# Layer 0's state-space scan in steps of 1024 elements, with B broadcast from DRAM and one shared decay bank

## The chip, the cores and the metric

The program runs on one NeuronCore of a Trainium2 chip. A core has five engines with an instruction stream each: TensorE (PE in the profile, its weight loads PEld), VectorE (DVE), ScalarE (ACT), GpSimd (POOL) and SyncE (SP, which here only issues transfers). They meet through semaphores. Operands lie in SBUF, and in PSUM, which has 8 banks of 128 x 512 float32. The metric is the time of one execution in microseconds (us), the lower the better.

## What is computed

The reference is a network of four layers on 4096 tokens (16 sequences of 256) of width 128. The change touches layer 0 alone, which adds a selective state-space scan and a mixture of experts to its input. The scan, cut to what matters:

```python
deltaA = jnp.exp(jnp.einsum('bld,dn->bldn', delta, A))          # decay
deltaB_u = (delta * u)[..., None] * Bm[:, :, None, :]           # input
def step(h, t):
    dA_t, dBu_t, C_t = t
    h = dA_t * h + dBu_t
    return (h, jnp.einsum('bdn,bn->bd', h, C_t))
y = ys + u * D
y = y * silu(res)
return y @ W_out + b_out
```

There are 256 channels d, 16 states n and 256 steps of time per sequence. The mixture sends each token to 2 of 16 experts with a capacity of 512; 12 of the experts are networks 128 to 512 to 128 with an exact GELU, and the results are gathered by token, weighted and added.

## The kernel before

Channels lie on the 128 partitions, in two halves c = 0, 1; time lies along the free axis. The function `mamba_front` (lines 338 to 588) makes u, delta, the gate (parked in DRAM as `gate_d`), and B and C for all tokens as three bf16 parts stacked on 96 partitions (`bc3`, the tile `bc` of the profile). Its last work is a row of scatters of tokens to the experts' buffers by GpSimd, the last seven of which wait for the logarithms of ScalarE (`ln_done`).

The function `mamba_scan` (lines 601 to 1021) walks over `NQ` = 128 steps q: 16 sequences b, and in each 8 pairs of states. A step has two units i, one for each half of the channels; a unit is 512 elements wide, 256 of time for each of the two states. For a unit

- ScalarE writes the decay to one of three PSUM banks (`decay`, L883), two instructions of 255 elements, since the first element of each state is 0 and makes the scan start anew;
- GpSimd multiplies delta*u by the spread B into `bu` (L746, a ring of 3), from `b_sb`, into which ScalarE has copied (L893) what TensorE spread over the partitions (L770) from the bf16 parts with a selection matrix;
- VectorE scans (L970) and multiplies by C (L976, tile `hc`), which TensorE has spread to bank 3 (L779);
- TensorE adds `hc` to the output's bank with an identity (L794, float32).

At the end of a sequence VectorE multiplies by the gate (L983), and TensorE projects (L807) and adds the residual (L808). The order of each engine's instructions is written out by hand, and the experts lie in the gaps of the same streams: expert e begins at step 7 + 6e (`FIRST`, `SPACING`), with a transposition (L845), two pairs of first-layer products (L837), each pair followed by its two GELUs on ScalarE (L914), the second layer (L820) and an addition by VectorE (L989). A GELU needs another activation table than the decay's exponential, so each pair of GELUs costs a table load before it and one after it. From step 84 on GpSimd also fetches 64 blocks of expert results by index (L731), nearly two a step; ScalarE weighs them (L924) and VectorE adds them (L999). SyncE issues the loads of weights, tokens and gates and the stores of results.

Both functions are printed here:

Of the kernel before, what the change touches and what calls it, by code (L numbers as in the profile page):

```python
# [6 lines left out]
F32 = mybir.dt.float32  # L7
# [330 lines left out]
def mamba_front(nc, g, t, u, gate_d, delta, bc3, r, disp, ybuf, scattered, f):  # L338
# [10 lines left out]
    with section(nc, "front", *ROUTE, "xz_ready", "gate_ready", "gate_out0", "gate_out1", "act_done", "biased",  # L349
                 "b_out_in", "near_in", "delta_in", "dt_ready", "dtx_done", "z_ready", "zb_done", "high_done", "rem_done",  # L350
                 "copied", "split_done", "abs_done", "exp_done", "ln_done", "delta_done", "neg_a") as s:
# [7 lines left out]
        rem = s.sb("rem", [KBC, 2, CH])  # L359
        with ExitStack() as early:  # L360
# [4 lines left out]
        gate_out = (s.gate_out0, s.gate_out1)  # L365

# [15 lines left out]
        with nc.Block() as block:  # L382

            @block.sync
            def _(sp):
                for dst, src in ((w_dt_in, "m_w_dt_in"), (w_bc, "m_w_bc"), (w_dt, "m_w_dt"), (b_dt, "m_b_dt")):
                    sp.dma_start(dst[:], t[src]).then_inc(s.delta_in, 16)
# [8 lines left out]
                for b in range(BATCH):  # L396
                    sp.wait_ge(s.gate_ready, b + 1)
                    sp.dma_start(gate_d[:, :, b * T:(b + 1) * T], gate[:, b % 2]).then_inc(gate_out[b % 2], 16)
                for p in range(2):
                    sp.wait_ge(gate_out[p], BATCH // 2 * 16)  # L400
                sp.wait_ge(s.near_in, 64)
# [199 lines left out]
def mamba_scan(nc, g, t, u, gate_d, delta, bc3, sel, disp, ybuf, r, scattered, f):  # L601

    PAIRS = DS // 2
    NQ = BATCH * PAIRS
    NU = NQ * DC
    DA, C_BANK, E0_BANK, BO, Y_BANK, E1_BANK = 0, 3, 4, 5, 6, 7
    RING = 3
    NE, CT = E0 - FIRST_MLP0, CAP0 // P
    W2, B1, B2, WN = FC * P, 2 * FC * P, 2 * FC * P + FC, 2 * FC * P + FC + D
    FIRST, SPACING = NT - SCATTERED_IN_FRONT + 3, 6  # L610
    TURN, UP0, UP1, DOWN0, DOWN1 = 0, 2, 4, 6, 7
    A_TURN, A_UP0, A_UP1 = 2, 4, 6
    GRP, SLOTS = 4, 4
    NGRP = NT // GRP
    Q_GATHER = FIRST + SPACING * (NE - 1) + 11
    Q_LAST = NQ - 3
    SKIP_BY_ACT = Q_GATHER // PAIRS + 1
    names = [f"gathered{j}" for j in range(NGRP)]
    with section(nc, "scan", *names, "skip_made", "skip_used", "zeroed", "du_ready", "b_ready", "b_copied", "bu_made",
                 "da_ready", "scan_done", "c_ready", "hc_ready", "sum_done", "yg_ready", "o_ready", "o_taken",  # L620
                 "gate_in0", "gate_in1", "ew_in0", "ew_in1", "ex_in0", "ex_in1", "turned", "xt_ready", "h_ready",
                 "act_done", "y_ready", "y_out", "stored", "weighted0", "weighted1", "combined") as s:
        a_neg, d_col, w_out = f.a_neg, f.d_col, f.w_out
        skip = s.sb("skip", [P, DC, T])
        exp_centre = s.sb("exp_centre", [P, 1])
        du = s.sb("du", [P, 2, DC, T])
        hc = s.sb("hc", [P, RING, 2, T])
        yg = s.sb("yg", [P, DC, T])
        gate = s.sb("gate", [P, 2, DC, T])
# [5 lines left out]
        free = g.xn_t[:].rearrange("p (k n t) -> p k n t", n=2, t=T)  # L635
        bu, b_sb, h = free[:, 0:3], free[:, 3:5], free[:, 5:7]
        gb = g.xn[:].rearrange("p (j k i) d -> p j k i d", j=SLOTS, k=2)
        gathered = s.sems[:NGRP]
        weighted, weighted_bank = (s.weighted0, s.weighted1), (E0_BANK, E1_BANK)
        gate_in, ew_in, ex_in = (s.gate_in0, s.gate_in1), (s.ew_in0, s.ew_in1), (s.ex_in0, s.ex_in1)  # L640

        def bank(i):
            return g.ps[:, i, :].rearrange("p (n t) -> p n t", t=T)
# [4 lines left out]
        def phase(q, offset):  # L648
            e, rest = divmod(q - FIRST - offset, SPACING)
            return e if rest == 0 and 0 <= e < NE else None  # L650

        def due(q):
            if q < Q_GATHER:
                return 0
            return min(2 * NT, -(-(q - Q_GATHER + 1) * 2 * NT // (Q_LAST - 4 - Q_GATHER)))

        def combined_at(q):
            return range(due(q - 3) // (2 * GRP), due(q - 2) // (2 * GRP)) if 0 <= q < NQ else range(0)

        last_groups = range(due(NQ - 3) // (2 * GRP), NGRP)  # L660

        with nc.Block() as block:

            @block.sync
            def _(sp):
                def load_gate(b):
                    if b >= 2:
                        sp.wait_ge(s.yg_ready, b - 1)
                    sp.dma_start(gate[:, b % 2], gate_d[:, :, b * T:(b + 1) * T]).then_inc(gate_in[b % 2], 16)
# [16 lines left out]

                load_gate(0)
                load_gate(1)
                load_weights(0)
                load_weights(1)  # L690
                sp.wait_ge(scattered, 2 * NT * 16)
                load_tokens(0)
                load_tokens(1)
                for q in range(NQ):
                    b, pr = divmod(q, PAIRS)
                    e = phase(q, TURN + 1)
                    if e is not None and e + 2 < NE:
                        load_tokens(e + 2)
                    e = phase(q, DOWN1 + 2)
# [4 lines left out]
                    if b >= 1 and pr == 2 and b + 1 < BATCH:  # L704
                        load_gate(b + 1)

            @block.gpsimd
            def _(pool):
                nc.gpsimd.memset(exp_centre[:], EXP_CENTRE).then_inc(s.zeroed, 1)

                def inputs(b):
                    to = slice(b * T, (b + 1) * T)
                    nc.gpsimd.tensor_tensor(du[:, b % 2], delta[:, :, to], u[:, :, to], ALU.mult).then_inc(s.du_ready, 1)

                def skip_term(b):
                    if b >= 1:
# [2305 lines left out]
```

## Time and profile before

| | |
|---|---|
| time, median of 3 runs | 1978.54 us (1978.04 to 1988.57) |
| span of the profiled execution, first to last instruction | 2006.6 us |
| what lies around that span | not recorded apart; the profiled span is itself 1.4% above the median |
| the scan's stage in the span | 179.4 to 792.9 us |
| DVE, PE, ACT, POOL busy in the whole span | 64%, 79%, 53%, 40% |
| mean granted TensorE clock | 0.890 |

The profile shows one execution. Busy time is the sum of an engine's instructions, and idle time is given with what ended it. In the trace a float32 matmul appears as two records, so 1024 records of L794 are 512 matmuls. The clock is a fraction of 2.4 GHz.

### The profile page before, as it was taken

What the parts mean: (1) busy time and instruction counts of PE and PEld (TensorE: products, weight loads), DVE (VectorE), ACT (ScalarE), POOL (GpSimd) and SP (SyncE); (2) the same over time, 40 slices, a digit from 0 to 9 for tenths busy, and PEclk for the clock granted to TensorE, in tenths of its full rate; (3) what the DMA queues carried; (4) which work ended last, traced back from release to release, by engine and by line L of the source; (5) the groups of instructions that cost most, each with busy time, mean ns of one, the idle gap of its engine ahead of it and who ended that gap; (6) DMA issues with size and microseconds to landing.
All of it is one profiled execution on the core that took longest, in us unless ns stands there. A gap on an engine that the chain in (4) does not pass through costs nothing. (4 is left out here: it accounts for less than half of the span.)

```text
span 2006.6 us, 34124 instructions
## 1 busy us (share of the span) xinstructions
PE 1593.7 (79%) x12145; PEld 1087.2 (54%) x12146; DVE 1288.1 (64%) x2309; ACT 1058.9 (53%) x1931; POOL 797.6 (40%) x809
## 2 busy tenths in 40 slices
PE   5993788888876776758889998965799999749974
PEld 5661566666654445535567765542344444638863
DVE  7525888788788888764534457758753896724334
ACT  1345787887776764434434444545454777314421
POOL 1447766565669994374212234431400000150041
PEclk9996899999998889658989999987699999569987
DMA  5211011111001110665321124314531341211311
GB/s 151 89 56 44 22 50 56 35 49 50 28 20 35 30 29 23 229 182 88 64 57 59 59 57 81 63 25 131 103 67 42 50 67 17 95 49 51 100 43 55
DMA packets 153335, 130.56 MB, mean 65 GB/s; under 512 B 18929, under 2 KB 137864, under 8 KB 152914
## 3 DMA queue, kind: packets, MB, share of 16 engines
q1 hardware_dynamic: 140554, 104.54, 21.1%
q0 software_dynamic: 12544, 23.82, 4.3%
q8 instruction: 100, 1.64, 0.4%
q14 instruction: 65, 0.53, 0.1%
q10 hardware_dynamic: 72, 0.03, 0.0%
HBM read 77.08 MB, written 52.43 MB: 65 GB/s over the span
## 5 line engine op out<-in xcount | busy, mean ns | idle before, releaser
L746 POOL TENSOR_TENSOR xn_t<-xn_t,scan_du 128x512 f32<-128x512 f32 x256 | 320.9, 1271 | 154.9 <-ACT xn_t L893 105.1
L970 DVE TENSOR_TENSOR_SCAN xn_t<-banks,xn_t 128x512 f32<-128x512 f32 x256 | 311.5, 1217 | 78.7 <-ACT banks L883 42.0
L794 PE MATMUL banks<-scan_hc,ident 128*128 128x256 f32 x1024 | 295.4, 414 | 49.1 <-DVE scan_hc L976 49.1
L2417 ACT ACTIVATE att_pr<-banks 128x768 f32<-128x768 f32 (+1 forms) x256 | 234.3, 917 | 161.9 <-PE banks L2309 76.1
L883 ACT ACTIVATE banks<-delta,scan_exp_centre,a_neg 128x255 f32<-128x255 f32 x512 | 265.0, 559 | 14.8 <-DVE xn_t L970 14.4
L794 PEld LDWEIGHTS banks<-scan_hc,ident 128*128 128x128 f32 x1024 | 193.7, 207 | 110.2 <-DVE scan_hc L976 70.1
L976 DVE TENSOR_TENSOR scan_hc<-xn_t,banks 128x512 f32<-128x512 f32 x256 | 175.8, 687 | 33.4 <-PE banks L779 14.3
L1030 POOL DMA_INDIRECT disp<-xn_tok,places x128 | 135.3, 1057 | 154.6 <-ACT att_pr L2417 44.2
L2325 PE MATMUL banks<-att_pr,att_vx 128*32 128x256 f32 (+1 forms) x2048 | 163.6, 383 | 19.0 <-issue 9.3
L2458 DVE TENSOR_REDUCE att_mb<-banks 128x6 f32<-128x768 f32 x128 | 121.1, 954 | 89.5 <-PE banks L2283 48.7
L2462 DVE TENSOR_REDUCE att_mb<-banks 128x4 f32<-128x1024 f32 x128 | 153.9, 1221 | 18.5 <-PE banks L2276 13.4
L2276 PE MATMUL banks<-att_ks,att_qs 48*128 48x256 bf16 (+1 forms) x1024 | 118.1, 281 | 45.0 <-DMA att_ks<-k_parts 31.2
L893 ACT COPY xn_t<-banks 128x512 f32<-128x512 f32 x128 | 74.5, 582 | 123.7 <-PE banks L770 92.2
L2301 PE MATMUL banks<-att_qs,att_ks 50*128 50x256 bf16 (+1 forms) x1024 | 111.0, 272 | 13.2 <-DMA att_qs<-att_mt 11.0
L1231 POOL IOTA gau_rev<- 128x8 f32 x1 | 0.1, 138 | 302.2 <-POOLq L76 302.2
L1415 POOL DMA_DIRECT2D ybuf<-att_yo x72 | 38.8, 539 | 156.7 <-DVE att_yo L1400 153.1
L1316 PE MATMUL banks<-grouped_w,att_xt 128*128 x288 | 98.4, 465 | 0.5 <-DVE att_xt L1382 0.3
L1605 POOL DMA_INDIRECT gau_gb<-ybuf,rows x32 | 32.2, 1007 | 146.0 <-DMA ybuf<-gau_eyo 136.6
L1365 ACT ACTIVATE att_a<-banks 128x352 f32<-128x352 f32 x72 | 33.4, 463 | 104.8 <-PE banks L1316 104.8
L2276 PEld LDWEIGHTS banks<-att_ks,att_qs 48*128 48x128 bf16 x1024 | 50.1, 101 | 64.2 <-issue 28.5
L779 PE MATMUL banks<-bc,state_sel 96*128 96x256 bf16 x256 | 53.0, 290 | 34.4 <-DVE scan_hc L976 27.7
L2325 PEld LDWEIGHTS banks<-att_pr,att_vx 128*32 128x32 f32 x2048 | 43.5, 110 | 66.0 <-issue 40.7
(384 smaller groups left out, 3339.2 us busy)
## 6 DMA issues: line engine op xcount, KB each, us to landing
scan_ew<-f_packed SPq DMA_DIRECT2D x12, 578.0 KB
q_parts<-att_p_parts SPq DMA_DIRECT2D x16, 384.0 KB, 4.7
k_parts<-att_p_parts SPq DMA_DIRECT2D x16, 384.0 KB, 6.1
att_qs<-q_parts SPq DMA_DIRECT2D x64, 96.0 KB
att_ks<-k_parts SPq DMA_DIRECT2D x64, 96.0 KB
gau_ew<-f_packed SPq DMA_DIRECT2D x8, 578.0 KB
disp<-zeros SPq DMA_DIRECT2D x1, 4608.0 KB, 15.4
att_xin<-disp SPq DMA_DIRECT2D x72, 64.0 KB
```

Of the source, the lines that this page charges most:

```text
L746: nc.gpsimd.tensor_tensor(bu[:, i % RING], b_sb[:, q % 2], du[:, b % 2, c:c + 1, :].to_broadcast([P, 2, T]), ALU.mult).then_inc(s.bu_made, 1)
L794: ins = nc.tensor.matmul(bank(Y_BANK)[:, c, :], g.ident[:], hc[:, i % RING, n, :], start=False, stop=(i % (PAIRS * DC) == PAIRS * DC - 1 a ...
L883: ins = nc.scalar.activation(bank(DA + i % RING)[:, n, 1:T], delta[:, c, b * T + 1:(b + 1) * T], ACT.Exp, scale=a_neg[:, c, state:state + ...
L970: v.tensor_tensor_scan(rows(h[:, i % 2]), g.ps[:, DA + i % RING, :], rows(bu[:, i % RING]), 0.0, ALU.mult, ALU.add).then_inc(s.scan_done, 1)
L976: v.tensor_tensor(hc[:, i % RING], h[:, i % 2], bank(C_BANK), ALU.mult).then_inc(s.hc_ready, 1)
L1030: pool.indirect_dma_start(disp, bass.IndirectOffsetOnAxis(ap=r.scat_i[:, k, i:i + 1], axis=0), src[:, i, :], None, bounds_check=disp.shape ...
L2276: ins = nc.tensor.matmul(g.ps[:, 2 * m_slot(i) + half, lo:hi], qs[rows_of, p, j, q * P:(q + 1) * P], ks[rows_of, p, j, 0:hi - lo], start=T ...
L2301: ins = nc.tensor.matmul(g.ps[:, 2 * s_slot(i) + half, k * T:k * T + T - q0], ks[rows_of, p, j, k * P:(k + 1) * P], qs[rows_of, p, j, q0:T ...
L2325: ins = nc.tensor.matmul(g.ps[r * 32:(r + 1) * 32, O_BANK, q0:T], vx[:, b % 2, k, 4 * jg + r, :], pr[:, i % RING, half, k * T:k * T + T - q0],
L2417: nc.scalar.activation(pr[:, i % RING], g.ps[:, at:at + 2, 0:W], ACT.Exp, scale=scale).then_inc(s.p_ready, 1)
L2458: v.tensor_reduce(mb[:, b % 2, j, :].rearrange("p (g n) -> p g n", g=2), g.ps[:, at:at + 2, 0:W].rearrange("p g (n k) -> p g n k", k=P), A ...
L2462: v.tensor_reduce(mb[:, b % 2, j, :], g.ps[:, at:at + 2, :].rearrange("p g (n k) -> p (g n) k", k=T), AX_X, ALU.max).then_inc(s.m_taken, 1)
```

## The change

The steps are cut the other way. A step k of 128 now is one state for two sequences (`PASS` = 512 columns of time) and for both halves of the channels at once, 1024 elements wide, in 8 passes of 16 states. One scan, one product with C, one product of GpSimd and two decays of 2 x 255 elements serve a step, where before there were two, two, two and four.

- B no longer goes through TensorE and ScalarE. The front copies the float32 rows of B from PSUM (`b_row`, one more ScalarE copy for each of 8 chunks) and SyncE stores them to `b_d` in DRAM. In the scan SyncE loads row n for each step, broadcast to 128 partitions (256 KB, 128 such loads, a ring of 4).
- C is still spread by TensorE from its bf16 parts, in one matmul of 512 columns; VectorE reads it for both halves with a step of 0.
- A step's two decays need two adjacent banks. Even steps use banks 0 and 1, odd ones banks 1 and 2, so bank 1 is shared: its decay for step k+1 waits until scan k is over, and scan k+1 waits for it. The other decay is made a step ahead.
- The skip term u*D is added by TensorE with a diagonal matrix (L801), in place of products on GpSimd and ScalarE and one on TensorE (L787).
- The experts are spaced 4 steps apart. The first two hidden blocks are parked in SBUF with `Identity` and get their GELU together with the other two, so that one table round trip serves an expert. The bias of the second layer is a matmul with a row of ones (L874), and ScalarE takes the result out (L928), not VectorE.
- The fetches are one a step, at steps 57 to 120; the weighted rows stay in SBUF, TensorE adds them (L835, L839), and ScalarE takes the sums out.

The core of the diff:

```diff
+                def store_b(ch):
+                    sp.wait_ge(s.b_saved, ch + 1)
+                    sp.dma_start(b_d[:, cols(ch)], b_row[:, ch % 2, :]).then_inc(b_out_done[ch % 2], 16)
...
                 def high(ch):
                     act.wait_ge(s.dt_ready, ch + 1)
+                    if ch >= 2:
+                        act.wait_ge(b_out_done[ch % 2], ch // 2 * 16)
+                    nc.scalar.copy(b_row[:, ch % 2, :], g.ps[0:DS, bc_bank(ch), :]).then_inc(s.b_saved, 1)
...
+    FIRST, SPACING = 7, 4
...
+                def load_b(k):
...
+                    if k >= B_RING:
+                        sp.wait_ge(s.bu_made, k - B_RING + 1)
+                    sp.dma_start(b_sb[:, k % B_RING, :], b_d[n:n + 1, cols(p)].to_broadcast([P, PASS])
+                                 ).then_inc(b_in[k % B_RING], 16)
...
+                    pool.wait_ge(b_in[k % B_RING], (k // B_RING + 1) * 16)
+                    if k >= BU_RING:
+                        pool.wait_ge(s.scan_done, k - BU_RING + 1)
+                    nc.gpsimd.tensor_tensor(bu[:, k % BU_RING], du[:, p % 2],
+                                            b_sb[:, k % B_RING, None, :].to_broadcast([P, DC, PASS]),
+                                            ALU.mult).then_inc(s.bu_made, 1)
...
+                    if GATHER <= k < GATHER + 2 * NT:
+                        fetch(k - GATHER)
...
+                def sum_states(k):
...
+                    pe.wait_ge(s.hc_ready, k + 1)
+                    for c in range(DC):
+                        ins = nc.tensor.matmul(g.ps[:, Y_BANK + c, :], g.ident[:], hc[:, k % 2, c, :], start=False,
+                                               stop=(n == DS - 1))
...
-                    for n in range(2):
-                        state = 2 * pr + n
-                        ins = nc.scalar.activation(bank(DA + i % RING)[:, n, 1:T], delta[:, c, b * T + 1:(b + 1) * T],
-                                                   ACT.Exp, scale=a_neg[:, c, state:state + 1], bias=exp_centre[:])
...
+                    bank = 2 * (k % 2) if own else SHARED
+                    c = bank - k % 2
+                    free_after = k - 1 if own else k
+                    if free_after >= 1:
+                        act.wait_ge(s.scan_done, free_after)
...
+                for k in range(NK):
+                    decay(k, False)
+                    decay(k + 1, True)
+                    if k >= 1:
+                        expert(k - 1)
...
+                    dve.wait_ge(s.da_ready, 2 * k + 2)
+                    dve.wait_ge(s.bu_made, k + 1)
+                    v.tensor_tensor_scan(rows(h[:, k % 2]), da_pair(k), rows(bu[:, k % BU_RING]), 0.0, ALU.mult,
+                                         ALU.add).then_inc(s.scan_done, 1)
```

ScalarE around one expert, before. `scan_eht` are the hidden blocks and `scan_ext` the transposed tokens; L883 is the decay, L893 the copy of B:

```order
L905 COPY scan_ext<-banks 128x512
L883 ACTIVATE banks<-delta,scan_exp_centre,a_neg 128x255 x2
L893 COPY xn_t<-banks 128x512
L883 ACTIVATE banks<-delta,scan_exp_centre,a_neg 128x255 x6
L897 COPY x_tok<-banks 128x256
L893 COPY xn_t<-banks 128x512
L914 ACT_TABLE_LOAD
L914 ACTIVATE scan_eht<-banks,scan_ew 128x512 x2
L883 ACT_TABLE_LOAD
```

The same place in the changed kernel. L913 is the decay, L941 the parked blocks, L947 and L950 the GELUs, L928 the expert's result:

```order
L934 COPY scan_ext<-banks 128x512
L913 ACTIVATE banks<-delta,scan_exp_centre,a_neg 128x2x255 x2
L941 ACTIVATE scan_eht<-banks,scan_ew 128x512 x2
L913 ACTIVATE banks<-delta,scan_exp_centre,a_neg 128x2x255 x2
L947 ACT_TABLE_LOAD
L947 ACTIVATE scan_eht<-banks,scan_ew 128x512 x2
L950 ACTIVATE scan_eht<-scan_eht 128x1024
L913 ACT_TABLE_LOAD
L913 ACTIVATE banks<-delta,scan_exp_centre,a_neg 128x2x255 x2
L928 COPY scan_eyo<-banks 128x512
```

Both tables are now loaded once per expert, with three GELUs between the loads where there were two; the next decays stand behind the second load.

TensorE over one expert in the changed kernel (L792 spreads C, L809 adds the states, L851 transposes, L863 and L869 are the first layer, L874 and L878 the second):

```order
L792 MATMUL banks<-bc,state_sel 128x512
L809 MATMUL banks<-scan_hc,ident 128x512 x2
L851 MATMUL banks<-ident,scan_exin 128x128 x4
L792 MATMUL banks<-bc,state_sel 128x512
L809 MATMUL banks<-scan_hc,ident 128x512 x2
L863 MATMUL banks<-scan_ext,scan_ew 128x512 x2
L792 MATMUL banks<-bc,state_sel 128x512
L809 MATMUL banks<-scan_hc,ident 128x512 x2
L869 MATMUL banks<-scan_ext,scan_ew 128x512 x2
L792 MATMUL banks<-bc,state_sel 128x512
L809 MATMUL banks<-scan_hc,ident 128x512 x2
L874 MATMUL banks<-scan_ew,ones_row 128x512
```

The sixteen matmuls of L878 follow. The whole expert stands within four steps, where before its pieces were spread over eight, the last two of them beside the next expert's first.

GpSimd in the gather phase of the changed kernel (L774 is the product with B, L758 a fetch, L748 a piece of delta*u):

```order
L774 TENSOR_TENSOR scan_bu<-scan_du,xn_t 128x1024
L758 DMA xn_tok<-ybuf,rows 128x128
L774 TENSOR_TENSOR scan_bu<-scan_du,xn_t 128x1024
L748 TENSOR_TENSOR scan_du<-delta,u 128x512
L758 DMA xn_tok<-ybuf,rows 128x128
```

One fetch stands behind each product, over 64 steps.

## Rows read from the trace of the kernel before

**Rows 1.** Windows of the stage with the scans alone: length, DVE busy (count), clock, DMA

```profile
275.00:560.00 285.00, 144.50 (x119) 0.96 0.14 43
580.00:767.00 187.00, 95.02 (x78) 0.87 0.11 29
767.00:789.00 22.00, 13.36 (x11) 1.00 0.00 1
```

**Rows 2.** The page's costliest groups that belong to the scan

```profile
L746 POOL TENSOR_TENSOR xn_t<-xn_t,scan_du 128x512 f32<-128x512 f32 x256 | 320.9, 1271 | 154.9 <-ACT xn_t L893 105.1
L970 DVE TENSOR_TENSOR_SCAN xn_t<-banks,xn_t 128x512 f32<-128x512 f32 x256 | 311.5, 1217 | 78.7 <-ACT banks L883 42.0
...
L883 ACT ACTIVATE banks<-delta,scan_exp_centre,a_neg 128x255 f32<-128x255 f32 x512 | 265.0, 559 | 14.8 <-DVE xn_t L970 14.4
...
L976 DVE TENSOR_TENSOR scan_hc<-xn_t,banks 128x512 f32<-128x512 f32 x256 | 175.8, 687 | 33.4 <-PE banks L779 14.3
...
L893 ACT COPY xn_t<-banks 128x512 f32<-128x512 f32 x128 | 74.5, 582 | 123.7 <-PE banks L770 92.2
```

**Rows 3.** Groups by form over the whole span: other widths, GELUs, table loads

```profile
L2000 DVE TENSOR_TENSOR att_p_rem<-att_p_y,att_p_parts 128x1024 f32<-128x1024 f32 x16 | 19.4, 1216 | 7.0 <-issue 3.9 <-ACT att_p_parts L2032 3.1
...
L2881 POOL TENSOR_TENSOR w_taps<-w_in_sb,w_taps 128x1024 f32<-128x1024 f32 x1 | 2.3, 2338 | 7.1 <-DMA w_taps<-m_taps 7.1
...
L2417 ACT ACTIVATE att_pr<-banks 128x1024 f32<-128x1024 f32 x128 | 130.6, 1023 | 49.1 <-PE banks L2301 47.4
...
L914 ACT ACT_TABLE_LOAD x24 | 30.8, 1283 | 0.4
...
L914 ACT ACTIVATE scan_eht<-banks,scan_ew 128x512 f32<-128x512 f32 x48 | 30.3, 683 | 0.3
```

**Rows 4.** Timeline at the stage's end, VectorE: start, us, engine, line

```profile
783.23 1.22 DVE L970 TENSOR_TENSOR_SCAN xn_t<-banks,xn_t 128x512 f32<-128x512 f32 x1
...
785.09 1.22 DVE L970 TENSOR_TENSOR_SCAN xn_t<-banks,xn_t 128x512 f32<-128x512 f32 x1
...
788.19 0.69 DVE L976 TENSOR_TENSOR scan_hc<-xn_t,banks 128x512 f32<-128x512 f32 x1
...
792.49 0.37 ACT L897 COPY x_tok<-banks 128x256 f32<-128x256 f32 x1 [8.81 <-PE banks L808]
```

**Rows 5.** Timeline of one pair of GELUs, ScalarE and VectorE

```profile
329.45 1.26 ACT L914 ACTIVATE scan_eht<-banks,scan_ew 128x512 f32<-128x512 f32 x2
...
330.74 1.28 ACT L883 ACT_TABLE_LOAD   x1
...
332.03 1.05 ACT L883 ACTIVATE banks<-delta,scan_exp_centre,a_neg 128x255 f32<-128x255 f32 x2
...
333.12 1.22 DVE L970 TENSOR_TENSOR_SCAN xn_t<-banks,xn_t 128x512 f32<-128x512 f32 x1 [1.36 <-ACT banks L883]
```

**Rows 6.** Timeline of TensorE at full clock (starts give the pace)

```profile
402.28 0.38 PE L779 MATMUL banks<-bc,state_sel 96*128 96x256 bf16 x2
402.50 1.03 PE L794 MATMUL banks<-scan_hc,ident 128*128 128x256 f32 x4
403.37 0.38 PE L770 MATMUL banks<-bc,state_sel 96*128 96x256 bf16 x2
```

**Rows 7.** Timeline of GpSimd: a fetch behind a product

```profile
641.29 1.04 POOL L731 DMA_INDIRECT xn_tok<-ybuf,rows  x1 [0.16 <-issue]
```

**Rows 8.** Timeline at the end of the front and the stage's start

```profile
172.96 0.97 POOL L1030 DMA_INDIRECT disp<-xn_tok,places  x1 [0.30 <-issue]
...
183.94 1.22 DVE L970 TENSOR_TENSOR_SCAN xn_t<-banks,xn_t 128x512 f32<-128x512 f32 x1 [4.36 <-POOL xn_t L746]
```

**Rows 9.** Loads by line: KB each, median us to landing

```profile
scan_exin<-disp SPq DMA_DIRECT2D x12, 256.0 KB, 2.9
```

**Rows 10.** The broadcast load of `b_out`, 64 KB, by its tile

```profile
DMA to landing us min/median/max: 3.9/3.9/3.9
```

More of the change, by code:

```diff
@@ L620, in mamba_scan @@
+    TURN, UP0, UP1, DOWN = 0, 1, 2, 3
+    GELUS = 3
+    GRP, SLOTS = PASS // P, 4
+    PROJECT = 3
+    STORED_AFTER = 2
+    GATHER = FIRST + SPACING * (NE - 1) + DOWN + 3
+    WEIGH = GATHER + 2 * GRP + 2
+    SCATTERED_HERE = NT - SCATTERED_IN_FRONT
+    names = [f"gathered{j}" for j in range(NPASS)]
+    with section(nc, "scan", *names, "zeroed", "diag_made", "du_ready", "b_in0", "b_in1", "b_in2", "b_in3", "bu_made",
                  "da_ready", "scan_done", "c_ready", "hc_ready", "sum_done", "yg_ready", "o_ready", "o_taken",
@@ L755, in _ @@
                         scatter(nc, pool, scattered, g.xn, disp, r, 2, range(i, i + 1))
[L756 to L757 removed]
+                    if n in (6, 10) and p + 1 < NPASS:
+                        inputs(p + 1, (6, 10).index(n))
+                    if GATHER <= k < GATHER + 2 * NT:
+                        fetch(k - GATHER)
             @block.tensor
             def _(pe):
[L761 to L772 removed]
@@ new lines, in _ @@
+                for k in range(NK):
+                    spread_c(k)
+                    if k >= 1:
+                        sum_states(k - 1)
+                    expert(k)
+                    p = projected_at(k)
+                    if p is not None:
+                        residual(p)
+                        project(p)
+                    j = combined_at(k)
+                    if j is not None:
+                        combine(j)
+                sum_states(NK - 1)
+                residual(NPASS - 1)
@@ new lines, in take_out, with expert @@
+                def take_out(p):
+                    act.wait_ge(s.o_ready, p + 1)
+                    nc.scalar.copy(rows(g.x[:, p * GRP:(p + 1) * GRP, :]), g.ps[:, E1_BANK, :]).then_inc(s.o_taken, 1)
+                def expert(k):
+                    e = phase(k, DOWN)
+                    if e is not None:
+                        act.wait_ge(s.y_ready, e + 1)
+                        if e >= 1:
+                            act.wait_ge(s.stored, e * 16)
+                        nc.scalar.copy(rows(eyo[:]), g.ps[:, E1_BANK, :]).then_inc(s.y_out, 1)
+                    e = phase(k, TURN)
@@ L953, in _, with take_sum @@
-                for j in combined_at(NQ - 1):
-                    weigh(j, 1)
-                for j in last_groups:
-                    for k in range(2):
-                        weigh(j, k)
-                take_out(BATCH - 1)
+                    ins.then_inc(s.weighted, 1)
+                def take_sum(j):
+                    act.wait_ge(s.x_sum, j + 1)
+                    nc.scalar.copy(rows(g.x[:, j * GRP:(j + 1) * GRP, :]), g.ps[:, E0_BANK, :]).then_inc(s.combined, 1)
+                decay(0, True)
@@ new lines, in _ @@
+                for k in range(NK):
+                    decay(k, False)
+                    decay(k + 1, True)
+                    if k >= 1:
+                        expert(k - 1)
+                        p = projected_at(k - 1)
+                        if p is not None:
+                            take_out(p)
+                        j = combined_at(k - 1)
+                        if j is not None:
+                            take_sum(j)
+                    due = weighed_at(k)
+                    if due is not None:
+                        weigh(*due)
@@ L960, in _ @@
+                for k in range(NK, WEIGH + 2 * GRP * NPASS):
+                    due = weighed_at(k)
+                    if due is not None:
+                        weigh(*due)
+                take_out(NPASS - 1)
             @block.vector
```

483 lines of the change are left out of this document (194 added, 289 removed).

## The prediction

> **What bounds the kernel now.** I read the windows first, to see the pace of the scan's stage, then the costliest groups for what a step costs each engine, then the timeline for what ends the waits.
>
> The stage has three paces. VectorE does two scans a step. Beside the experts 119 scans take 285 us, 4.79 us a step; beside the fetches 78 take 187 us, 4.79 again; in the last steps, with neither, scans start 1.86 us apart, 3.72 a step [rows 1, 4]. VectorE needs 1217 + 687 ns a unit [rows 2], so only those last steps are bound by it. From the first scan (183.94) to the end of the last product (788.88) are 604.9 us for 128 steps, 4.73 each [rows 4, 8]; at VectorE's own pace they would be 476.
>
> What stands in between differs. Beside the experts, ScalarE: around a pair of GELUs stand two table loads of 1.28 us, and a scan waits for the decay behind them (1.36 us of idle VectorE at 333.12) [rows 3, 5]. Beside the fetches, GpSimd: two products of 1271 ns and nearly two fetches, each 0.16 + 1.04 us, are about 4.9 us [rows 2, 7]. TensorE is no bound: a spread of B or of C takes 0.22 us, the sums of a unit 0.86 [rows 6], 2.2 us of a step and 7.7 us more per expert over six steps.
>
> **The change part by part.** Sizes first, each from the nearest row.
>
> - A product of VectorE on 1024 elements takes 1216 ns, 529 more than on 512 [rows 2, 3]. No scan of another width is in the trace; I let it grow by twice that, two passes over the same columns, so to 1217 + 1060 = 2.28 us. The step then is 1.86 + 0.53 + 1.06 = 3.45 us. If a width doubled all of a scan's time it would be 3.6; the other end is 3.4.
> - GpSimd's product on 1024 takes 2338 ns, against 2 x 1271 [rows 2, 3].
> - A decay of 2 x 255: ScalarE's slope from 512 to 1024 is (1023 - 582)/512 = 0.86 ns an element [rows 2, 3], so 559 + 220 = 0.78 us, and in a row of several 0.74, since 512 of them now take 265.0 us, 0.52 each [rows 2]. Bounds 0.56 and 1.12.
> - TensorE's work is by columns: 512 of float32 cost 0.86 us, 512 of bf16 0.22 [rows 6]. A step now has 0.22 + 2 x 0.86 = 1.94.
>
> *Plain steps.* 124 steps by 3.45 are 427.8. VectorE loses its combining and its experts' additions to TensorE and ScalarE. The seven gate products inside the stage are 1.17 each (1216 less the overlap seen in the pace), 8.2. The wait on the shared bank costs nothing in a plain step: the decay (0.78) runs under the product with C (1.2), with 0.4 to spare. If that cover goes, ScalarE's delay goes into the scan one for one, and that is what happens at the experts.
>
> *First four steps.* GpSimd has two scatters behind each product, 2.34 + 2 x 1.25 = 4.84, so 19.4.
>
> *Experts.* Let the scan of the step in which an expert is transposed (F) end at 0. At 3.45 a step, scan F+2 ends at 6.9 and ScalarE starts: two decays to 8.4, table to 9.7, two GELUs of 0.63 [rows 5] to 10.9, the one of 1024 (as 1023 ns [rows 3]) to 12.0, table to 13.3, and only then the shared decay, to 14.05. Scan F+4 was due at 11.5. It is 2.55 late. TensorE meanwhile may start the second layer only after the GELUs, at 12.0: one product of 0.86 and sixteen of 0.21 end at 16.3, and C for step F+4 comes at 16.5, when its scan has ended (16.3). TensorE's work for an expert is 4 x 1.94 + 0.85 + 3.4 + 4.3 = 16.3 against VectorE's 13.8, so it carries its lag on, and going through the second and third expert by the same steps I get cycles of 16.8 to 17.1. I take 3.1 over 13.8 for each of 12: 37. Inside this stretch TensorE also has three projections (2.6 each) and three skip terms (1.7), 13 us, partly in the gap ahead of its second layer; I take 5. Bounds for the two: 18 (a stall of 1.5) and 75 (6).
>
> *Fetches.* GpSimd: 2.34 + 1.20 + two delta*u products of 1.29 in 16 steps (0.16) and some dispatch, 3.74 a step, against VectorE's 3.45 + 0.07. Over 64 steps 13.8 more. The ring of three would lend it two steps, but the first fetch waits for the last expert's store, which leaves about 1.6: I take 12. Bounds 0 and 25 (0.4 a step).
>
> *B's transfers.* 128 loads of 256 KB on SyncE's queue. A plain load of 256 KB lands in 2.9 us [rows 9]. A load is issued about three steps ahead, 10 us, so it is hidden; even behind a blocked store of an expert's result I find some 4 us to spare. Cost nothing; without the cover it would be a wait of GpSimd at each step.
>
> *Removed.* B's spreads (0.22 us a step on TensorE) and its copies (74.5 us of ScalarE [rows 2]) and half of the table loads (24 of 48). Their gain is in the shorter steps, not counted again.
>
> *Edges.* Start: two delta*u (2.5), two small products for the diagonal (1.2 at most), one product (2.3) are 6.1 from the block's start at 179.4 to the first scan, against 4.5: +1.6. End: before, 792.86 - 788.88 = 4.0 from the last product to the last copy [rows 4]; now sums 1.8, residual and two blocks 2.6 (over the gate product), projection 1.7, copy 0.6: 6.8, +2.8. Front: eight more copies of about 0.57 on ScalarE. Those within its main loop lie in waits for TensorE; three stand ahead of the logarithms for which the last scatters wait, and those scatters end the front at 173.93 [rows 8]: +1.5, bounds 0 and 4.6.
>
> *Sum.* 19.4 + 427.8 + 8.2 + 37 + 5 + 12 = 509.4, against 604.9: -95.5. Edges +5.9. Net -89.6 us in a span of 2006.6, so 1917.0. The profiled span is longer than the median of the runs, 1978.5; in that proportion (0.986) the change is -88, so **1890 us**.
>
> **A rule against it.** The trace puts the decay right behind a table load: load at 330.74, 1.28 us, decay at 332.03, and the load right behind the GELUs, which end at 330.71 [rows 5]. The Trainium skill ("ScalarE: Activation LUTs", What ACT_TABLE_LOAD costs) gives every switch a drain of about 1380 ns on top, 2.66 us in total. By the row the two loads cost 2.6 us per expert; by the page 5.3, and with the page's figure the sum would be 33 us higher, near 1923. The trace does not agree with it.
>
> **Rivals.**
> 1. *The experts stall twice as long.* TensorE is at 16.3 of 16.9 us there, and each stretch at half clock (the windows show 0.96 there and 0.87 later [rows 1]) goes straight into the end. For: two engines are late at once. Against: a busier TensorE has kept 1.00 in the last steps. Stall 6 us: +35, **1925**. Chance 0.13.
> 2. *No stall worth the name*: decays and GELUs overlap more than I have them, and GpSimd keeps up with the fetches. -25 to -45, **1855**. For: ScalarE's instructions overlap in the trace (0.52 pace on 559). Against: the two loads are a fixed 2.6. Chance 0.10.
> 3. *B's broadcast loads are the bound; slower than before.* All 128 partitions read one row in DRAM. The only broadcast load here took 3.9 us for 64 KB, more than a plain load of 256 KB [rows 9, 10]. If loads come no faster than one in T, the stage is 128 x T once T passes 4.0, and the gain is gone at T = (509 + 90)/128 = 4.7 us. At T = 6 the stage is 768: **2145**. At four times the 3.9 us it would be 15.6. Against: that load stood in the start's crowd, and what it shows is landing, not rate; four can be under way. Chance 0.07.
> 4. *The steps don't shorten* (a scan of 1024 costs two of 512 and the shared bank adds its decay each step): 3.8 a step, +45, **1935**. It speaks against this that the decay is shorter than the product that covers it. Chance 0.03.
> 5. *Each change of table also drains ScalarE.* A pause as long as a load (1.28) behind each of the two would be 12 x 2.56 = +31, **1921**. The row above shows none (0.01 us). It is the page's rule, in the kernel's terms. Chance 0.02, since a wider last GELU could show what a narrow one hides.
>
> **Numbers.** My forecast holds 0.65, from 1865 to 1915. The range goes to 1858 and 1925, which takes in most of rivals 1 and 2. A change of less than 0.5% (10 us) is about what a measurement of this kernel cannot tell from none. Faster by more: my case and rivals 1, 2, 4, 5, less a little for what I have not seen, 0.90. Slower by more: rival 3 and that remainder, 0.07. Within: 0.03.
>
> **What would show it.** After: 128 scans near 2.28 us and products near 1.216; steps 3.45 apart outside of experts and fetches; idle time of VectorE ahead of the scan, ended by the decay, once per expert and 2 to 3 us long, about 37 in all; GpSimd nearly without idle time from step 57 to 120 at 3.7 us a step; SyncE's loads of B landing in about 3 us and no wait of GpSimd for them; 24 table loads fewer; a stage of about 516 us. I am wrong if GpSimd waits for B's loads, if scans of 1024 take over 2.4 us, or if the stalls at the experts exceed 6 us.

## The result and the profile after

| | before | after |
|---|---|---|
| median of runs taken side by side | 1978.29 us (1975.38 to 1988.57, 4 runs) | 1902.7 us (1890.76 to 1918.67, 4 runs) |
| ratio, with its 95% interval | | 0.9599 (0.9543 to 0.9655) |
| the profiled execution | span 2006.6 us | time 1890.76 us, span 1889.0 us |
| from the stage's first instruction to its last copy | 613.4 us | 531.1 us |
| of that, first scan to the end of the last product | 604.9 us | 517.3 us |
| mean granted TensorE clock, whole span | 0.890 | 0.909 |

The change is faster by 4.0%, 76 us between the medians. The forecast was 1890 us (-4.5%, -88 us), in a range of 1858 to 1925. A second set of five runs gave a ratio with a tighter interval, 0.9576 (0.9557 to 0.9594); it stands first among the experiments.

The costliest groups of the page after (busy time, mean ns of one, idle time before them); they answer to [rows 2]:

```profile
L774 POOL TENSOR_TENSOR scan_bu<-scan_du,xn_t 128x1024 f32<-128x1024 f32 x128 | 301.8, 2361 | 97.5 <-DVE xn_t L1002 93.8
L1002 DVE TENSOR_TENSOR_SCAN xn_t<-banks,scan_bu 128x1024 f32<-128x1024 f32 x128 | 292.6, 2286 | 49.6 <-ACT banks L913 32.2
...
L913 ACT ACTIVATE banks<-delta,scan_exp_centre,a_neg 128x510 f32<-128x510 f32 x256 | 189.6, 772 | 175.9 <-DVE xn_t L1002 163.9
...
L1010 DVE TENSOR_TENSOR scan_hc<-xn_t,banks 128x1024 f32<-128x1024 f32 x128 | 156.2, 1220 | 22.2 <-PE banks L792 18.9
```

A scan of 1024 costs 2286 ns where 512 cost 1217, and the 256 decays of 2 x 255 take 189.6 us where 512 of 255 took 265.0. ScalarE's idle time ahead of the decays is now a wait for a scan to free a bank (163.9 us), which is harmless where the decay still fits under the product with C.

The windows of the stage with the scans alone (length, busy time and count, clock, DMA share, GB/s), as in [rows 1]: the steps beside the experts, those beside the fetches, the last ones.

```profile
207.00:431.80 224.80, 114.20 (x50) 1.00 0.43 118
431.80:673.70 241.90, 148.65 (x65) 0.96 0.33 95
673.70:691.00 17.30, 11.41 (x5) 1.00 0.05 18
```

Divided by their counts, these are 4.50, 3.72 and 3.46 us a step. The same stretch beside the experts with every engine shows TensorE busy for 215.68 us of 224.80, at full clock. One expert from the timeline (start, duration, engine, line, idle time before and what ended it). It follows a sequence's projection, so two of its steps (3.65 and 6.30 us) are 0.2 and 0.3 longer than in a cycle that doesn't:

```profile
272.60 2.28 DVE L1002 TENSOR_TENSOR_SCAN xn_t<-banks,scan_bu 128x1024 f32<-128x1024 f32 x1
...
273.27 1.28 ACT L947 ACT_TABLE_LOAD   x1
...
274.56 1.27 ACT L947 ACTIVATE scan_eht<-banks,scan_ew 128x512 f32<-128x512 f32 x2
...
275.72 1.05 ACT L950 ACTIVATE scan_eht<-scan_eht 128x1024 f32<-128x1024 f32 x1
276.79 1.28 ACT L913 ACT_TABLE_LOAD   x1
...
277.88 3.84 PE L878 MATMUL banks<-scan_ew,scan_eht 128*128 128x128 f32 x32
278.09 1.48 ACT L913 ACTIVATE banks<-delta,scan_exp_centre,a_neg 128x510 f32<-128x510 f32 x2
278.90 2.29 DVE L1002 TENSOR_TENSOR_SCAN xn_t<-banks,scan_bu 128x1024 f32<-128x1024 f32 x1 [2.56 <-ACT banks L913]
...
281.55 0.38 PE L792 MATMUL banks<-bc,state_sel 96*128 96x512 bf16 x1
...
282.03 1.22 DVE L1010 TENSOR_TENSOR scan_hc<-xn_t,banks 128x1024 f32<-128x1024 f32 x1 [0.83 <-PE banks L792]
```

The reader sees both stalls of the prediction. From 273.27 to 278.09 ScalarE is busy with its two table loads and the three GELUs between them, and the scan waits 2.56 us for the decay behind them. Then VectorE waits another 0.83 us for C, which stands on TensorE behind the second layer. A step is counted from the start of one scan to the start of the next. The steps of a cycle without a projection or skip term (here called plain) are 3.45, 3.46, 6.00 and 4.26 us, 17.17 together, against 13.8 for four plain ones.

VectorE's waits in the stage, 170 to 700 us (total, times, longest):

```profile
DVE xn_t L1002 <- ACT banks L913: 32.2, 19, 2.6
...
DVE scan_hc L1010 <- PE banks L792: 18.9, 26, 1.6
DVE xn_t L1002 <- POOL scan_bu L774: 16.3, 11, 6.6
```

### The profile page after: what moved, and what is told of

It reads as the page before. It is cut to its first block and busy times, and to the rows that moved or that the text cites. A ratio compares the mean times of both kernels' runs of the same rounds, so it can differ in the third digit from the quotient of the medians.

```text
span 1889.0 us, 31228 instructions
## 1 busy us (share of the span) xinstructions
PE 1516.4 (80%) x11272; PEld 938.9 (50%) x11272; DVE 1243.2 (66%) x2017; ACT 914.7 (48%) x1544; POOL 761.4 (40%) x661
## 5 line engine op out<-in xcount | busy, mean ns | idle before, releaser
L774 POOL TENSOR_TENSOR scan_bu<-scan_du,xn_t 128x1024 f32<-128x1024 f32 x128 | 301.8, 2361 | 97.5 <-DVE xn_t L1002 93.8
L1002 DVE TENSOR_TENSOR_SCAN xn_t<-banks,scan_bu 128x1024 f32<-128x1024 f32 x128 | 292.6, 2286 | 49.6 <-ACT banks L913 32.2
L913 ACT ACTIVATE banks<-delta,scan_exp_centre,a_neg 128x510 f32<-128x510 f32 x256 | 189.6, 772 | 175.9 <-DVE xn_t L1002 163.9
L809 PE MATMUL banks<-scan_hc,ident 128*128 128x512 f32 x512 | 250.2, 612 | 1.3 <-DVE scan_hc L1010 1.3
L2451 DVE TENSOR_REDUCE att_mb<-banks 128x6 f32<-128x768 f32 x128 | 121.3, 955 | 77.6 <-PE banks L2276 39.4
L1010 DVE TENSOR_TENSOR scan_hc<-xn_t,banks 128x1024 f32<-128x1024 f32 x128 | 156.2, 1220 | 22.2 <-PE banks L792 18.9
L2318 PE MATMUL banks<-att_pr,att_vx 128*32 128x256 f32 (+1 forms) x2048 | 156.1, 373 | 13.5 <-ACT att_ot L2415 6.5
L809 PEld LDWEIGHTS banks<-scan_hc,ident 128*128 128x128 f32 x512 | 100.9, 197 | 86.8 <-issue 80.1
L792 PE MATMUL banks<-bc,state_sel 96*128 96x512 bf16 x128 | 50.8, 397 | 115.3 <-DVE scan_hc L1010 91.2
L792 PEld LDWEIGHTS banks<-bc,state_sel 96*128 96x128 bf16 x128 | 12.5, 98 | 180.0 <-DVE scan_hc L1010 149.2
L2294 PEld LDWEIGHTS banks<-att_qs,att_ks 50*128 50x128 bf16 x1024 | 39.9, 94 | 69.4 <-issue 40.6
```

The source lines that it names most:

```text
L774: nc.gpsimd.tensor_tensor(bu[:, k % BU_RING], du[:, p % 2], b_sb[:, k % B_RING, None, :].to_broadcast([P, DC, PASS]), ALU.mult).then_inc(s ...
L809: ins = nc.tensor.matmul(g.ps[:, Y_BANK + c, :], g.ident[:], hc[:, k % 2, c, :], start=False, stop=(n == DS - 1))
L913: nc.scalar.activation(g.ps[:, bank, :].rearrange("p (b t) -> p b t", t=T)[:, :, 1:T], delta[:, c, cols(p)].rearrange("p (b t) -> p b t", ...
L1002: v.tensor_tensor_scan(rows(h[:, k % 2]), da_pair(k), rows(bu[:, k % BU_RING]), 0.0, ALU.mult, ALU.add).then_inc(s.scan_done, 1)
L1010: v.tensor_tensor(hc[:, k % 2], h[:, k % 2], g.ps[:, C_BANK, None, :].to_broadcast([P, DC, PASS]), ALU.mult).then_inc(s.hc_ready, 1)
L2294: ins = nc.tensor.matmul(g.ps[:, 2 * s_slot(i) + half, k * T:k * T + T - q0], ks[rows_of, p, j, k * P:(k + 1) * P], qs[rows_of, p, j, q0:T ...
```

## The experiments

Ratios are taken against the kernel before on the same chip. Its median was 1978 us beside the result above, 1879 us on the chip of experiments 1 to 4, 1881 on that of 5 to 8 and 1997 on that of 9 and 10. What I compare is the length of the scan's stage, which hardly depends on the set of runs: in experiment 1 it is within 1.6 us of the first profile, although the kernel takes 100 us less there. "Scans" is the time from the start of the first to the start of the last one, 513.75 us in the first profile after.

**1. The changed kernel again**, unedited, five runs.

> The changed kernel itself once more, in five rounds with the kernel before. Its profiled scan stage took 517.3 us from the first scan to the last product where 509.4 were worked out; the medians differ by 76 us where the two stages in the traces differ by 83. Theory: the stage is reproducible to 1 us and the gain of the whole is 80 to 88 us (ratio 0.956 to 0.960); the rest of a run's spread lies in the stages that the change doesn't touch. Rival: the new stage itself varies by 10 us or more from run to run (its loads from DRAM), and then a second profile shows another length of the stage.

Measured: 1799.93 us (1797.59 to 1802.43) against 1879.44, ratio 0.9576. Scans 515.4 us. The stage repeats to 1.6 us although the whole span is 88 us shorter here (1800.7 against 1889.0). Of these 88, 4.3 lie ahead of the first scan (173.05 against 177.32) and the rest behind the stage, in layers that the change doesn't touch. The stage's own 1.6 us are one step of 5.89 instead of 4.27, behind the first expert's second layer:

```profile
218.10 5.47 PE L878 MATMUL banks<-scan_ew,scan_eht 128*128 128x128 f32 x32
```

It took 5.47 us and not 3.84, at a mean granted clock of 0.69: part of it ran at the lower of the clock's two levels, 1.2 GHz. In the first profile the clock stayed at 1.00 there. So a dip of the clock in a second layer does go straight into the step, as rival 1 has it, but it came once in twelve experts. Experiments 6 and 7 have the same dip and the same long step; the first profile and experiment 10 have neither.

**2. No table changes**: the GELUs become an identity.

```diff
-  nc.scalar.activation(eht[:, f, :], ..., ACT.Gelu, ...)
+  nc.scalar.activation(eht[:, f, :], ..., ACT.Identity, ...)
...
-  nc.scalar.activation(rows(eht[:, 0:2, :]), rows(eht[:, 0:2, :]), ACT.Gelu)
+  nc.scalar.activation(rows(eht[:, 0:2, :]), rows(eht[:, 0:2, :]), ACT.Identity)
```

> The experts' GELUs in the scan stage are computed as Identity, so the experts' outputs are wrong and 24 table loads (1.28 us each) are gone; everything else stays. A plain cycle of four steps with an expert takes 17.2 us in the trace, of which 13.8 are plain steps. Theory A (ScalarE's window and TensorE's 16.3 us of work per cycle hold the cycle together): the cycle falls only to 16.3 to 16.5, the stage by 8 to 15 us. Theory B (ScalarE's window alone): the cycle falls to 13.8 to 14, the stage by some 40. Theory C (TensorE alone): the cycle stays at 17.2, the stage unchanged.

**3. A light second layer**: 4 of its 16 matmuls (`for f in range(1)` for `range(FC)`).

> The experts' second layer uses one of its four hidden blocks: 4 matmuls of 128 columns and not 16, 2.6 us less work for TensorE per expert (wrong outputs of the experts); the table loads stay. Theory A: the cycle is then held by ScalarE's window alone, 13.8 + 2.55 = 16.3 to 16.5 us, and the projections and skip terms fit in the room, so the stage falls by 12 to 22 us. Theory B: the cycle stays at 17.2 and the stage falls by under 5. Theory C: the cycle falls to 13.8 to 14, the stage by 40 or more.

**4. Both of these together.**

> Both cuts together: no table loads at the experts and 4 matmuls in the second layer. All theories that put the experts' stalls on these two expect them gone: a cycle of 13.8 to 14 us, the stage shorter by 40 to 50 us, with idle time of VectorE ahead of its scans only in the first four steps. If the cycle stays over 15 us, a third cause (the waits between PE and ScalarE, or B's loads) is at work.

Measured, for the three:

| | time (one run; the first a median of five) | scans | steps of a plain expert cycle |
|---|---|---|---|
| as it is | 1799.93 | 515.4 | 3.45 3.46 6.00 4.26 |
| no tables | 1786.63 | 507.2 (-8.2) | 3.45 3.46 3.69 5.83 |
| light second layer | 1781.96 | 494.9 (-20.4) | 3.45 3.46 5.99 3.46 |
| both | 1766.31 | 475.5 (-39.9) | 3.45 3.45 3.46 3.45 |

VectorE's waits without the table loads:

```profile
DVE scan_hc L1010 <- PE banks L792: 33.9, 25, 2.4
DVE xn_t L1002 <- POOL scan_bu L774: 15.7, 10, 6.4
DVE xn_t L1002 <- ACT banks L913: 9.1, 19, 0.8
```

The stall did not go; it moved from the wait for ScalarE (32.2 to 9.1 us) to the wait for TensorE (18.9 to 33.9). Each engine is nearly late enough on its own, so that either alone gives 8 or 20 us and both together 40. That is more than the sum of the two (28.6), because taking one away only uncovers the other. With both gone a plain cycle is 13.8 us. All three cycles came as expected: 16.43 us without the tables and 16.36 with the light layer, each for 16.3 to 16.5, and 13.82 with both; the 39.9 us stand at the lower edge of the 40 to 50. The 1.6 us of the clock's dip in experiment 1 are in each of the three gains: against the first profile they are 6.5, 18.8 and 38.3, which changes nothing in the reading.

**5. The decay in SBUF**: a ring of three SBUF tiles in place of the PSUM banks, filled two steps ahead. It takes out the shared bank, and makes both operands of the scan come from SBUF.

```diff
+ da = s.sb("da", [P, DA_BANKS, DC, PASS])
...
- nc.scalar.activation(g.ps[:, bank, :]..., ACT.Exp, ...)
+ nc.scalar.activation(da[:, k % DA_BANKS, c, :]..., ACT.Exp, ...)
...
- v.tensor_tensor_scan(rows(h[:, k % 2]), da_pair(k), rows(bu[:, k % BU_RING]), ...)
+ v.tensor_tensor_scan(rows(h[:, k % 2]), rows(da[:, k % DA_BANKS]), rows(bu[:, k % BU_RING]), ...)
```

> The decays go to a ring of three SBUF tiles of 1024 and not to three PSUM banks, so no bank is shared and both decays of a step are made two steps ahead of its scan. Theory A: the wait on the decay behind the table loads goes away, TensorE's 16.3 us per cycle stay: the cycle of an expert falls from 17.2 to 16.3 to 16.5 us and the stage by 8 to 15, as without the tables. Rival (a rule of the Trainium skill, GPSIMD Engine Reference: GpSimd shares its SBUF interfaces with VectorE, with contention when VectorE has two SBUF inputs; the scan now has two): GpSimd's product grows from 2.36 us or the scan from 2.28 us, steps beside the fetches go from 3.59 to over 4 us and the stage is 20 us or more longer.

Measured: 1962.36 us (1956.04 to 1964.27) against 1880.9, ratio 1.0429 (1.0391 to 1.0468): slower than the kernel before. Scans 675.3 us. Groups of the stage, by form:

```profile
L1001 DVE TENSOR_TENSOR_SCAN xn_t<-scan_da,scan_bu 128x1024 f32<-128x1024 f32 x128 | 480.9, 3757 | 19.9 <-POOL scan_bu L775 19.9
L775 POOL TENSOR_TENSOR scan_bu<-scan_du,xn_t 128x1024 f32<-128x1024 f32 x128 | 301.6, 2358 | 125.8 <-DVE xn_t L1001 123.3 <-DMA xn_t<-b 0.6
...
L759 POOL DMA_INDIRECT xn_tok<-ybuf,rows x64 | 180.5, 2820 | 16.6 <-issue 10.0 <-DMA ybuf<-scan_eyo 6.5
```

The waits for ScalarE are indeed gone, but the scan takes 3757 ns in the mean, not 2286, and a fetch 2820 ns where it took 1044. GpSimd's product keeps its 2358 ns. The timeline at the stage's end shows what the scan's length goes with:

```profile
839.64 2.35 POOL L775 TENSOR_TENSOR scan_bu<-scan_du,xn_t 128x1024 f32<-128x1024 f32 x1 [2.29 <-DVE xn_t L1001]
840.67 3.47 DVE L1001 TENSOR_TENSOR_SCAN xn_t<-scan_da,scan_bu 128x1024 f32<-128x1024 f32 x1
...
845.31 2.28 DVE L1001 TENSOR_TENSOR_SCAN xn_t<-scan_da,scan_bu 128x1024 f32<-128x1024 f32 x1
```

The scan at 840.67 runs beside the last 1.32 us of a product of GpSimd and takes 3.47 us. The one at 845.31, when GpSimd has nothing left, takes 2.28, as with its decay in PSUM. So it isn't the SBUF operand by itself that costs, but that operand beside GpSimd. And the scan isn't slowed, it is held up. The product ends at 841.99 and the scan 2.15 us later, nearly its whole 2.28. So it is everywhere: of the 113 scans that overlap a product with B, 105 end 2.15 to 2.16 us after the product's end, whether they overlapped much or little; in the other 8 a piece of delta*u follows the product, and the scan ends 2.15 us after that. In the last steps the two simply take turns, and a step is 4.64 us, 2.36 and 2.28. Beside the fetches the scan holds up GpSimd in turn:

```profile
792.50 2.36 POOL L775 TENSOR_TENSOR scan_bu<-scan_du,xn_t 128x1024 f32<-128x1024 f32 x1
792.79 4.23 DVE L1001 TENSOR_TENSOR_SCAN xn_t<-scan_da,scan_bu 128x1024 f32<-128x1024 f32 x1
...
795.02 2.85 POOL L759 DMA_INDIRECT xn_tok<-ybuf,rows  x1 [0.16 <-issue]
```

The fetch is issued during the scan and ends 0.85 us after it; a piece of delta*u that starts during a scan is lengthened too (2.04 us in the mean, not 1.28). In the kernel with its decay in PSUM 102 scans overlap a product, and none takes over 2.29 us. Of the two outcomes expected, theory A missed and the rival held, with some 160 us in place of its 20 or more. The Trainium skill ("GPSIMD Engine Reference", Specifications, the row on SBUF interfaces) warns of such a contention when VectorE reads two inputs from SBUF; the run agrees: VectorE lost 1.2 us in this scan, and GpSimd lost time wherever the scan had started first; its product with B, which always went ahead of the waiting scan, lost nothing.

**6. Fetches off GpSimd**: SyncE loads blocks of `ybuf` in plain order in their place (so the gather by token is left out).

```diff
...
- pool.indirect_dma_start(gb[:, j % SLOTS, k, i % GRP, :], None, ybuf, ...)
+ sp.dma_start(gb[:, j % SLOTS, k, i % GRP, :], ybuf[n * P:(n + 1) * P, :])
```

> The 64 blocks are loaded by SyncE with plain transfers in order of address and not by GpSimd by index (wrong rows, the same bytes); GpSimd keeps only its products. Theory: beside the fetches GpSimd was the bound at 3.59 us a step and in the steps after its delta*u products; without them these steps fall to 3.46, and steps 57 to 121 lose 10 to 13 us. Rival: the longer steps there come from the combining on TensorE and ScalarE; then they stay and the stage changes by under 4 us.

Measured: 1786.56 us, scans 504.9 (-10.5). The steps beside the fetches fall to 3.45. The prediction had 12 for this term. What stays there over the plain steps and four gate products is 2.2 us, 1.9 of them in four waits of the scan for a decay in the steps behind a projection, for which the prediction had put nothing in this part.

**7 and 8. B's ring of 2, and of 1**, in place of 4 (`B_RING`).

> The ring of B's loads has two places and not four, so a load is issued when the product before the last is done. A load lands in 3.3 us and its issue takes 0.3. Theory: in plain steps the cover of a step (3.45 us and the 1.1 us that GpSimd waits) still just hides it; beside the fetches GpSimd loses 0 to 0.5 us a step, and at the experts SyncE, which waits for a result to be stored, delays the next load: in all 10 to 60 us longer. If the stage is the same within 3 us the loads have more cover than worked out.

> The ring of B's loads has one place: a load is issued when the product before it is done, so nothing of it is hidden. It measures what the cover is worth. Theory: GpSimd's step is 2.36 + 0.3 + 3.3 = 6.0 us, the stage 128 x 6.0 = 768 us or 250 us longer, and the kernel slower than before. Rival: without other loads in flight a broadcast of 256 KB lands faster, in 2.5 us or less, and the step is under 5.3.

Measured: with 2, 1796.17 us and scans 514.4, no change, though GpSimd waited 84.9 us for B in 30 places; that waiting is off the path, and I had expected 10 to 60 us of loss. With 1, 2015.18 us and scans 728.3 (+213). GpSimd's waits in the ring of one, and its product:

```profile
POOL scan_bu L774 <- DMA xn_t<-b: 305.3, 119, 5.1
...
L774 POOL TENSOR_TENSOR scan_bu<-scan_du,xn_t 128x1024 f32<-128x1024 f32 x128 | 300.1, 2344 | 326.5 <-DMA xn_t<-b 305.3 <-DVE xn_t L1002 12.7 <-issue 8.5
```

With nothing in front of it a broadcast load costs its landing (3.2 us in the median on this run's page): a step is 2.34 of product and 3.3 of load, 5.64 us, and 128 of them are 722. Expected were 6.0 us and a loss of 250. So rival 3's price T for loads one after the other is 3.3 us, below both the 3.45 of a step and the 4.7 from which it would have decided.

**9. The kernel before, on the chip with the longest times**, one run.

> The kernel before, with a profile on the chip of the experiments, where it takes 1880 us and not the 1978 of the first runs. Theory: the scan stage is the same as in the first trace, 604.9 us from the first scan to the last product within 3 us, and the 100 us lie in later layers, whose steps wait for transfers. Rival: the whole program runs slower by the same share there (5%), and the stage takes 575.

Measured: 2004.96 us, with 602.7 us from the first scan (181.17) to the start of the last (783.87). In the first trace the same stretch has 603.0: from 183.94 [rows 8] to the scan behind the two of [rows 4], which starts at 786.94. The stage before repeats within 0.3 us, as the stage after did within 1.6. The expectation was for the chip on which this kernel takes 1880 us, and the run fell to another, on which it takes 1997. So that the old stage, too, is as long where the kernel is 100 us faster isn't shown; the new one is, by experiment 1.

**10. The second layer starts earlier.** TensorE's bias and its products with the two hidden blocks that are ready first no longer wait for the wide GELU.

```diff
- pe.wait_ge(s.act_done, (e + 1) * GELUS)
+ pe.wait_ge(s.act_done, e * GELUS + 2)
...
- for i in range(CT):
-     for f in range(FC):
+ for pair in ((2, 3), (0, 1)):
+     if pair[0] == 0:
+         pe.wait_ge(s.act_done, (e + 1) * GELUS)
+     for i in range(CT):
+         for f in pair:
```

> The changed kernel with one wait split: the second layer's bias matmul and its eight products with the third and fourth hidden block start when their two GELUs are done, and only the other eight wait for the wide GELU. TensorE then never idles at the end of the table window and is done about 1 us earlier. Theory A: a plain cycle falls from 17.2 us to what ScalarE's window alone gives, 16.35, and the lag of TensorE at projections and skip terms is partly made up: the stage is 8 to 15 us shorter, ratio to before about 0.950. Rival: the wait for C behind the second layer was no part of the cycle, and the stage changes by under 3 us.

Measured: 1912.51 us against 1997.14, ratio 0.9585 (0.9552 to 0.9618), which can't be told from the 0.9576 of the change itself. Scans 508.8 us, 5.0 less than in the first profile (6.6 less than in experiment 1, 1.6 of them its dip of the clock), where I expected 8 to 15: a miss. In plain cycles the step behind the stall falls from 4.26 to 3.46 or 3.53. In the cycles with a projection or a skip term nearly nothing changes (6.02, 4.41, 5.02, 3.65, 6.29, 4.11), since there the GELUs were not what TensorE was late for: in the changed kernel TensorE idles 0.66 us or more ahead of the second layer in six of the twelve cycles, and 0.08 or nothing in the other six. VectorE's waits:

```profile
DVE xn_t L1006 <- ACT banks L917: 32.2, 19, 2.6
...
DVE scan_hc L1014 <- PE banks L792: 13.5, 20, 1.6
```

ScalarE's part is untouched, TensorE's falls from 18.9 to 13.5. Of the versions that leave nothing out it is the shortest in the stage, and in the whole program not measurably so.

## Why the prediction was right, and where it was off

| term of the sum | predicted | in the trace after |
|---|---|---|
| scan, product with C, decay, GpSimd's product | 2.28, 1.216, 0.78, 2.34 us | 2.286, 1.220, 0.772, 2.361 |
| a plain step | 3.45 | 3.45 to 3.46 |
| first four steps | 19.4 | 19.38 |
| twelve experts | 37 | 40.2 |
| projections and skip terms among them | 5 | 8.3 |
| fetches | 12 | 12.7 |
| first scan to last product | 509.4 | 517.3 |
| start, end | 6.1, 6.8 | 6.8, 7.0 |
| front | +1.5 | not seen |

- **Sizes and plain steps** came out to within a hundredth or two of a microsecond: the scan that no row showed did grow by two passes of a product over the same columns.
- **The mis-sized term is the experts.** A plain cycle is 17.17 us, not 16.9: 3.35 over 13.82, by 12 are 40.2. The steps 7 to 56 take 224.8 us; less 50 plain ones (172.8), three gates (3.5) and those 40.2, 8.3 are left for the three places where one pair of sequences ends and the next begins, with a projection and a skip term in two neighbouring cycles, 2.8 each, where I gave 5 for all. I had taken much of their 13 us as lying in TensorE's gap ahead of the second layer. TensorE is busy 96% there; experiment 4 shows 11.3 us of them even when nothing else is late (its steps 7 to 56 take 187.6 us; less 172.8 and 3.5). The mechanism, a stall first by ScalarE and then by TensorE, is shown by experiments 2 to 4.
- **Fetches**: products stood 3.59 us apart in the steps without a piece of delta*u (436.56, 440.16, 443.74). That GpSimd sets this pace is shown by experiment 6, which took away 10.5 us of the 12.7. The other 2.2 stay without the fetches, mostly as waits behind projections, which my sum had at nothing in this part. So the fetches alone were 10.5, and that the total came so near to 12 is a small piece of luck.
- **B's loads** are hidden as said. They landed in 3.3 us in the median, and GpSimd waited for them 1.8 us in all, 0.6 of it at the stage's start, where I had put nothing. Experiments 7 and 8 show how much cover there was: half the ring would do.
- **Edges**: the end is right. The front's 1.5 us can't be seen: from the start of the last matmul of its convolution to its last scatter were 38.0 us before and 37.1 after in the first profiles, 36.7 before and 36.9 after (experiments 9 and 10) on one chip. The changed kernel alone moves more than that, with 33.0 in experiment 1. So nothing over 1 us shows, and whether the three copies found room or drown in this scatter stays open.
- **Rivals.** 1 and 2 (a stall of 6 us, or none) fall by the wait of 2.56 + 0.83 us. One reason given against 1 was misread, though: in the last steps of the old stage, where the clock was at 1.00, TensorE was not busier but less busy (15.12 us of 22.00, against 240.50 of 285.00 beside the experts). It is the new profile that shows a clock of 1.00 with TensorE busy 96%. 3 falls by the 1.8 us of waits for loads, and by experiment 8. 4 falls by the plain step. 5 falls by the timeline: the wide GELU ends at 276.77, the load starts at 276.79 and takes 1.28 us, and the decay follows at 278.09, 0.02 us behind it. A page of the Trainium skill ("ScalarE: Activation LUTs", What ACT_TABLE_LOAD costs) has a drain of about 1380 ns for each; no load here shows one.
- **From the stage to the time.** Stage, start and end gave -87.6 + 2.3 + 3.0 = -82.3 us, against -91.1 (-95.5, +1.6, +2.8); with the front it is -83.2 against -89.6. Scaled by the prediction's 0.986 that is -82, or 1896.5 us and a ratio of 0.9585, which lies within both intervals. So 6.5 of the 12.7 us between forecast and median come from my sum; the other 6 lie within the scatter of these runs of the changed kernel (28 us), and I can't assign them. The two profiled spans by themselves differ by more, 117.6 us: 83.2 as above, 8.0 ahead of the end of the front's convolution, and 26.4 behind the stage (1213.7 us before, 1187.4 after). The last is in layers that the change leaves alone, and the 8.0 don't recur: on one chip (experiments 9 and 10) that convolution ends 2.0 us later in the changed kernel. I count neither as a gain. In experiment 1 the medians differ by 79.5 us, about what the stage gives.

What stays open: why the layers behind the scan take some 100 us more in one set of runs than in another. Between the first profile after and that of experiment 1 the attention of layer 1 and the gated layer behind it differ most (from the first to the last L2451, 429.4 us against 392.0; of L1661, 242.7 against 191.9), with waits that the profile puts down to transfers (37.6 us ahead of L2451, 41.2 ahead of L1870 and L1876) and that experiment 1 doesn't have. No run here tests it.

## What to carry to other kernels

Where two engines each feed a third one, work out for one cycle by when each is ready: with ScalarE 2.6 and TensorE 0.8 us late in one step, relieving one gave 8 or 20 us, and both 40. A wider step pays the fixed costs once (a plain step fell from 3.72 to 3.45 us). But the work that shares the streams (a pair of table loads with its GELUs, a second layer) then stands as one block that no longer fits under a single product: the experts took back 40 us, and projections and skip terms 8, of the 150 that steps at the plain pace would have gained (604.9 less 19.4, 427.8 and 8.2). Before an operand of VectorE is moved out of PSUM to free banks, so that both its inputs lie in SBUF, look at whether GpSimd works beside it. And when two engines look slow together, compare ends and not only lengths: a constant distance of 2.15 us between the ends showed that one was waiting for the other.

## What the runs showed of the hardware that I had not expected

- A scan of 128 x 1024 with both operands in SBUF takes 2.28 us beside an idle GpSimd and 3.47 us when it overlaps 1.3 us of a product there; in the mean of 128 it was 3.76. It ends 2.15 us after that product does, so the two take turns. With the decay in PSUM it is 2.28 to 2.29 throughout, beside products or not. GpSimd's indirect transfers stretched as well (1.04 to 2.82 us), and its pieces of delta*u (1.28 to 2.04), its product with B not at all (2361 and 2358 ns).
- One stretch at the lower clock in a second layer made it 5.47 us instead of 3.84 and the step behind it 5.89 instead of 4.27 (experiment 1).
- A load that broadcasts one row of 2 KB to 128 partitions lands in 3.3 us, hardly more than a plain load of the same 256 KB (2.9, [rows 9]).
- The kernel before took 1879, 1881, 1978 and 1997 us (medians) in four sets of runs, at least three of them on different chips, with the scan's stage equal within 0.3 us in the two profiles of it, at 1978 and 1997.
